# Attention in two float32r pieces, two heads in the row halves of TensorE, with the small steps of a group moved

## The reference

```python
# x: 8 sequences x 512 rows x 256; 16 heads of DH = 16
qkv = (x @ Wqkv).reshape(b, l, 3, H, DH)
q = q * cos + rotate_half(q) * sin          # the same for k
scores = einsum('bqhd,bkhd->bhqk', q, k) * DH ** -0.5
attn = softmax(scores, axis=-1)
out = einsum('bhqk,bkhd->bqhd', attn, v).reshape(b, l, d)
x = layernorm(x + out @ Wo)
x = layernorm(x + ffn(x))                   # shared expert + 2 of 8 experts
```

## Time and profile before

| | |
|---|---|
| Profiled execution, span of its instructions | 1291.3 us |
| Median of the three timed runs | 1292.8 us |
| PE / DVE / ACT / POOL busy over the span | 95% / 76% / 77% / 45% |
| Attention, from the first instruction to the last group | 0 to about 566 us |
| One group in the main loop | 64.06 us for four, 16.0 us each |
| Granted PE clock in the main loop | 0.99 to 1.00 |

### The profile page before, as it was taken

One profiled execution on the slowest core, in us unless ns is written; L12 is line 12 of the kernel. 1 busy time (PEld: TensorE's weight loads), 2 busy tenths in 40 slices (PEclk: granted clock), 3 DMA queues, 4 the chain that ended last, 5 costly groups with the idle time before them and its releaser, 6 DMA issues. The chain is left out here.

```text
span 1291.3 us, 29542 instructions
## 1 busy us (share of the span) xinstructions
PE 1224.3 (95%) x9440; PEld 934.5 (72%) x9440; DVE 976.6 (76%) x1925; ACT 996.4 (77%) x2043; POOL 583.9 (45%) x590
## 2 busy tenths in 40 slices
PE   4899999999999999979899969999999999999997
PEld 3444444444444444337899969999999999999897
DVE  6888887888788888728676648777777777777596
ACT  6699998999899999846654437777777777777687
POOL 6332322232223220005467745666666666666763
PEclk8899999999999999988899979999999999999999
DMA  9300000010000000433022246777777777776363
GB/s 298 117 19 19 18 19 20 2 35 3 19 2 19 2 18 3 144 104 117 18 91 100 87 158 197 260 251 253 246 238 238 235 249 253 253 239 217 101 218 119
DMA packets 125414, 161.28 MB, mean 125 GB/s; under 512 B 17088, under 2 KB 108224, under 8 KB 125312
## 3 DMA queue, kind: packets, MB, share of 16 engines
q1 hardware_dynamic: 118496, 141.25, 33.7%
q0 software_dynamic: 6816, 18.75, 4.1%
HBM read 122.06 MB, written 37.52 MB: 124 GB/s over the span
## 5 line engine op out<-in xcount | busy, mean ns | idle before, releaser
L546 DVE TENSOR_REDUCE att_mx<-att_psA 128x1 f32<-128x512 f32 x512 | 337.8, 683 | 75.5 <-PE att_psA L331 74.9
L461 ACT ACTIVATE att_prob<-att_psB 128x512 f32<-128x512 f32 x512 | 299.7, 600 | 54.0 <-PE att_psB L341 41.0
L341 PE MATMUL att_psB<-att_qk 128*128 128x512 bf16 x512 | 197.6, 388 | 12.8 <-issue 5.6
L1648 ACT ACTIVATE exp_psU<-exp_psU,ew_b 128x256 f32<-128x256 f32 x312 | 126.6, 447 | 103.7 <-PE exp_psU L1605 103.7
L331 PE MATMUL att_psA<-att_qk 96*128 96x512 bf16 x512 | 196.9, 386 | 3.0 <-DVE att_mx L546 3.0
L1699 DVE CAST exp_hh<-exp_psU 128x512 fp32r<-128x512 f32 x156 | 107.9, 692 | 101.9 <-ACT exp_psU L1648 101.9
L1588 PE MATMUL exp_psD<-exp_w2h,exp_hh 128*128 128x256 f32 x624 | 175.8, 282 | 0.0
L1603 PE MATMUL exp_psU<-exp_xh,exp_w1h 128*128 128x256 f32 x624 | 173.7, 278 | 1.4 <-DVE exp_xl L1690 1.4
L1605 PE MATMUL exp_psU<-exp_xh,exp_w1l 128*128 128x256 f32 x624 | 173.4, 278 | 0.0
L1604 PE MATMUL exp_psU<-exp_xl,exp_w1h 128*128 128x256 f32 x624 | 173.3, 278 | 0.0
L1589 PE MATMUL exp_psD<-exp_w2l,exp_hh 128*128 128x256 f32 x624 | 172.4, 276 | 0.0
(11 more groups left out here) (215 smaller groups left out, 3244.9 us busy)
## 6 DMA issues: line engine op xcount, KB each, us to landing
ew_w<-ew SPq DMA_DIRECT2D x40, 1024.0 KB, 6.1
exp_w<-ew SPq DMA_DIRECT2D x38, 1024.0 KB, 5.8
slots_x<-pre_acc SPq DMA_DIRECT2D x13, 780.0 KB, 10.8
pre_spare<-slots_x SPq DMA_DIRECT2D x39, 260.0 KB, 4.1
out_g<-rows_y SPq DMA_DIRECT2D x32, 256.0 KB, 4.1
ew_b<-eb SPq DMA_DIRECT2D x39, 128.0 KB
pre_spare<-xT SPq DMA_DIRECT2D x8, 512.0 KB, 4.5
attn_rows<-att_ob SPq DMA_DIRECT2D x8, 512.0 KB, 2.8
```

What stands on the lines that cost most here:

```text
L341: pe.matmul(psB[B_BANK[n % U]][:, :], r[:, 1, kt * P:(kt + 1) * P], r[:, 0, :], start=True, stop=True).then_inc(s_bmm, 1)
L461: act.activation(prob[:, n % PR, :], psB[B_BANK[n % U]][:, :], ACT.Exp, scale=SCALE).then_inc(s_exp, 1)
L546: dve.reduce_max(mx[:, g % 2, n % U:n % U + 1], psA[A_BANK[n % U]][:, :], AX_X).then_inc(s_max, 1)
```

## The change

The score operands become two float32r pieces (high and low), with three products of pieces, 3 x 16 = 48 rows, and the maximum in two pieces in rows 48 and 49 of the half. Two heads lie in the two halves of the 128 partitions (rows 0 to 63 and 64 to 127), so that a score product uses 64 rows of the array. In each unit the column product uses one half and the row product the other. A transposing step now turns a pair of heads, q or k, in four float32r products with a float32r identity (`turn_pair`), once in four units, and ACT copies 512 columns of it (`copy_pair`). POOL makes both pieces; the casts on DVE and the `spread` on ACT are gone. `split_max` is gone: `turn_max` transposes the maxima as float32, and `copy_max` cuts them in two on DVE, in two instructions, the second of which waits for the first. `place_max` issues four DMAs in place of three. The output has one buffer where it had two. The table of units is another, and the order in which psX is handed on is another.

```diff
-    TERMS = 6
+    TERMS = 3
     KR = TERMS * DH
+    PIECES = 2
+    KC = KR + PIECES
+    HALF = P // 2
-    PROJECT_QK, ROPE, COPY_OUT, TURN_OUT, NORM_OUT = (0, 1), (1, 2, 3), 3, 5, (5, 6)
-    PROJECT_V, COPY_V, SPLIT_MAX, TURN_MAX, COPY_MAX = 13, 13, 8, 10, 9
+    PROJECT_QK, TURN_MAX, TURN_OUT, PROJECT_V = (0, 4), 8, 10, 12
+    ROPE, COPY_MAX, NORM_OUT = (5, 6, 7), 9, (11, 12)
+    COPY_OUT, COPY_V, SPLIT_X = 4, 14, 12
...
+        qk = a.sb("qk", [P, RING, 2, PAIRS, L], F32R)
...
             def score_rows(n, it):
-                g, h, qt = n // U, n // NT, n % NT
+                g, u = n // U, n % U
+                pair, qt, j = u // (2 * NT), u // 2 % NT, 1 - u % 2
...
-                r = qk[0:KR, g % RING, :, h % G]
+                r = qk[half_of(j):half_of(j) + KR, g % RING, :, pair]
             def score_cols(n, it):
                 kt, j = u // G, u % G
...
-                r = qk[:, g % RING, :, j]
+                r = qk[half_of(j):half_of(j) + KC, g % RING, :, j // 2]
...
+            def turn_pair(k, it):
...
                 for t in range(NT):
+                    at = ((t * 2 + i) * H + h) * HALF
+                    m = pe.matmul(psT[:, t * P:(t + 1) * P], stack[:, b % 2, at:at + P], ident[:, :], start=True, stop=True)
+                m.then_inc(s_tmm, 1)
...
-                    last = {QK: (s_vev, p + V_LEAD, 1), OUT: (s_qrd, p + QK_LEAD + 1, 1),
-                            MAX: (s_onrm, p, 1), VALUE: (s_mev, p + 2, 1)}[use]
+                    last = {QK: (s_vev, p + V_LEAD, 1), MAX: (s_qrd, p + QK_LEAD + 1, 1),
+                            OUT: (s_mev, p + 2, 1), VALUE: (s_onrm, p, 1)}[use]
...
             def turn_max(g, it):
-                wait(pe, it, s_msp, g + 1, 1)
-                pe.matmul(psX[0:PIECES * U, 0:P], mstk[:, :, :].rearrange("p m u -> p (m u)"), ident[:, :], start=True, stop=True).then_inc(s_mtr, 1)
+                wait(pe, it, s_max, U * (g + 1), U)
+                pe.transpose(psX[:, 0:P], mx[:, g % 2, :], identf[:, :]).then_inc(s_mtr, 1)
...
             def place_max(g, it):
                 for k in range(PIECES):
+                    for j in range(2):
+                        row = half_of(j) + KR + k
...
             def copy_max(g, it):
-                dve.tensor_copy(mrow[:, g % 2, :], psX[0:PIECES * U, 0:P]).then_inc(s_mev, 1)
+                link(dve.tensor_scalar(mrow[:, g % 2, 0, :], psX[0:U, 0:P], -1.0, None, ALU.mult))
+                linked(it)
+                dve.scalar_tensor_tensor(mrow[:, g % 2, 1, :], psX[0:U, 0:P], -1.0, mrow[:, g % 2, 0, :].bitcast(F32),
+                                         ALU.mult, ALU.subtract).then_inc(s_mev, 1)
...
+            def split(tile, it):
...
+                    pool.tensor_tensor(rr[:, tile % 2, :], rc[:, :], rs[:, :], ALU.add).then_inc(s_rr, 1)
+                    for i in range(2):
+                        write_high(b, t, i, lambda out, *sides: pool.tensor_tensor(out, *sides, ALU.add), rc, rs).then_inc(s_hi, 1)
+                for i in range(2):
+                    wait(pool, it, s_hi, 2 * tile + i + 1, 2)
+                    pool.tensor_tensor(low(b, t, i), heads_of_part(rr[:, tile % 2, :], i), stacked(b, t, i)[:, :, 0:DH].bitcast(F32),
+                                       ALU.subtract).then_inc(s_lo, 1)
```

More of the change, by code:

```diff
@@ L152, in attention @@
         s_onrm = a.sem("o_normed")
[L153 to L156, removed]
+        s_ost = a.sem("o_stored")
+        s_tmm = a.sem("pair_turned")
+        s_tev = a.sem("pair_ready")
         s_mtr = a.sem("max_turned")
@@ L203, in heads_of, with stacked, half_of, high @@
             return t[:, :].rearrange("p (h d) -> p h d", d=DH)
-        def terms(stack, b, t):
-            return stack[:, b % 2, t].rearrange("p i h (m d) -> p (i h) m d", d=DH)
+        def stacked(b, t, i):
+            at = (t * 2 + i) * H * HALF
+            return stack[:, b % 2, at:at + H * HALF].rearrange("p (h m) -> p h m", m=HALF)
+        def half_of(j):
+            return HALF * (j % 2)
+        HI = ((0, 16), (0, 32))
+        LO = (32, 16)
+        def high(b, t, i):
+            first, second = HI[i]
+            return stacked(b, t, i)[:, :, first:second + DH].rearrange("p h (m d) -> p h m d", d=DH)[:, :, ::second // DH, :]
+        def low(b, t, i):
+            return stacked(b, t, i)[:, :, LO[i]:LO[i] + DH]
+        def heads_of_part(v, i):
+            return v[:, i * D:(i + 1) * D].rearrange("p (h d) -> p h d", d=DH)
+        def write_high(b, t, i, op, *sources):
+            return op(high(b, t, i), *(heads_of_part(v, i).unsqueeze(2).to_broadcast([P, H, 2, DH]) for v in sources))
         block = pr.block
@@ L461, in exps, with copy_pair @@
                 act.activation(prob[:, n % PR, :], psB[B_BANK[n % U]][:, :], ACT.Exp, scale=SCALE).then_inc(s_exp, 1)
-            def copy_head(h, it):
-                g = h // G
-                wait(act, it, s_tmm, h + 1, G)
-                act.activation(qk[0:KR, g % RING, :, h % G, :], psT[0:KR, :, :], ACT.Copy).then_inc(s_tev, 1)
+            def copy_pair(k, it):
+                g, pair, i = k // G, k % G // 2, k % 2
+                wait(act, it, s_tmm, k + 1, G)
+                act.activation(qk[:, g % RING, i, pair, :], psT[:, :], ACT.Copy).then_inc(s_tev, 1)
             def copy_out(g, it):
@@ L524, in period @@
                         copy_v(p + V_LEAD, it)
-                    if u == SPREAD and valid(p + QK_LEAD - 1, NT * B):
-                        spread(p + QK_LEAD - 1, it)
             groups(act, period)
@@ L601, in rope @@
                     wait(dve, it, s_rr, tile, 1)
+                    if tile > FILL:
+                        wait(dve, it, s_hi, 2 * tile, 2)
                     dve.tensor_tensor(heads_of(rc), x, table(cos, 0, DH), ALU.mult)
@@ L633, in _, with period @@
             dve.wait_ge(s_tab, 32)
-            def fill(tile):
+            def period(p, it):
+                tile = p + QK_LEAD
                 if tile < FILL:
@@ L654, in period @@
                         row_max(n + A_LEAD, it)
[L655 to L660 removed]
+                    if u in ROPE and valid(tile, NT * B):
+                        rope(tile, ROPE.index(u), it)
+                    if u == COPY_MAX and valid(p + 1, NG):
+                        copy_max(p + 1, it)
                     if u in NORM_OUT and valid(p - 1, NG):
                         norm_out(p - 1, NORM_OUT.index(u), it)
[L663 to L667 removed]
             def after_loop():
```

236 lines of the change are left out of this document (83 added, 153 removed).

## The result

The change makes the kernel 12.5% slower: 1458.8 us (median of four runs, 1441.6 to 1468.6) against 1293.0, a ratio of 1.125 [1.118, 1.131]. The forecast was 1331 us with a range up to 1375, so the direction was right and the size was missed by 128 us. The profiled execution spans 1457.1 us.

What follows compares the result with a forecast made beforehand. PE was taken as the bound, 16.1 us a group. The psX chain +31, store +14 and filling -6.5 gave +38.5 on 1291.3 us, 1330; the median, 1.5 higher, made it 1331 us, 8-in-10 range 1253 to 1375.

Steps and rivals of the forecast that it cites:

- PE's sum: PE's work per attention group: falls from 16.1 to 13.5 us, with 0.25 us for a pair of score products.
- the filling: Start of the kernel: first transpose at about 24 us, first column product some 6.5 us earlier (2 to 8).
- The chain through psX: Attention: four successive uses of psX make PE wait 3.7 us a group, 17.2 us a group in all, +31 us.
- The three waits: PE waits about 1 us each a group: output's transpose for maxima copy, v projection for norm_out, maxima's transpose for rope.
- the walk: Step-by-step timing of one attention period's hand-overs: PE works 13.5 us and waits 3.7, 17.2 us a group.
- Granted clock still near 1.00: Sign that the forecast is right: PE's granted clock stays near its full level.
- the slow clock: Rival: PE runs slow after each of seven store waits, some 4 us more each, +28, 1359 us; chance 0.07.
- The placing of the maxima behind the store: SP's queue in seven store periods: maxima land 2.0 us too late and block PE's first column product, +14 us.
- The halves do not overlap: Rival: a pair of score products costs 0.46 us, a group 18.8 us, +82, 1375 us; chance 0.17.
- PE's sum rules: Rival: waits in attention overlap more, so a group follows PE's work at 14.2 us, 1253 us; chance 0.17.

Runs made afterwards that it cites:

- e8: Kernel e1 with every score product over all 128 rows instead of half of them: 1300.3 us, ratio 1.007 to the kernel before.
- e5: Changed kernel with every score product over all 128 rows, same order and instructions: 1385.3 us, ratio 1.073 to the kernel before.
- e1: Changed kernel with half rows kept, but the units and psX order of the kernel before: 1307.4 us, ratio 1.016 to the kernel before.
- e9: Kernel e5 with the placing of the maxima ahead of the output store in SP's order: 1379.0 us, ratio 1.068 to the kernel before.
- e7: Changed kernel with the placing of the maxima ahead of the output store in SP's order: 1456.8 us, ratio 1.118 to the kernel before.
- e3: Kernel e1 with each unit's row product in the same row half as its column product: 1729.0 us, no ratio given.
- e2: Changed kernel with PE's waits filled: unit 10's row product issued five times, unit 12's turn three times: 1457.3 us, ratio 1.128 to the kernel before.
- e12: Changed kernel with the readers of psX ahead of each unit's row maximum on DVE: 1357.9 us, ratio 1.043 to the kernel before.

## Why the prediction was off, step by step

The medians split the loss into three steps: the float32r pieces in full rows and the old order, +10 us (e8 against the 1290.5 of before beside it); the order of psX at full clock, +85 (e5 against e8); the half rows in that order, +74 (after against e5). They sum to 168, against 166 measured, since before's own median moved from 1293.0 to 1290.5. The split depends on the order in which it is made: with the old order of psX the half rows cost 7 us (e1 against e8), not 74. The forecast had -72 for PE's sum and the filling, +110 for the chain and the store, and nothing for the clock.

- **The chain through psX: right.** The three waits are where the walk put them, 0.42, 1.08 and 1.02 us at full clock (the last in the wait list as 1.0). It gave 3.7 us of waiting a group; the order costs 3.0 (e5 against e8). The 2.5 us that PE's smaller sum was to pay back of them were not there.
- **PE's sum: the first step that failed, by the charge for borders.** I took 0.25 for a pair and 13.5 us a group; e1 has about 16. The price of the pair itself was right, 0.23 to 0.25 in a stream, and for the reason given, overlap, though the choice within 0.22 to 0.46 rested on column strips alone. What was mis-sized is the change of tile shape. I charged it for the turns only, eight changes and 0.6 us a group in all. It falls due wherever a half-row pair stands beside a full-array product, on both sides: e1 has twelve stays in the half rows (one or two pairs in a row), so that its sixteen pairs come to 6.1 us (8 x 0.43 + 4 x 0.67) in place of 4.0 and some 0.4 that the sum held with the products with V, and the full-array steps pay as well: q and k cost 0.84 to 0.90 in place of 0.7, the output's transpose 0.56 in place of 0.45. For v the new sum used 0.7, where the old sum had read 0.9 from the rows; it is 0.92. The rule of the Trainium skill, "TensorEngine Tiling (Array Packing)", section Key Properties, which I weighed in the prediction, was right in both halves: the tiles do run side by side, and a change of mode costs time, about 0.1 us on each side of a border in these traces. In the changed kernel's own order, with eight stays, I add the period from 261.62 to 280.48 up to 14.8 us of work, an estimate from the distances between starts; the other 4.1 of its 18.9 us are the three waits and smaller ones for exponents. The walk had 13.5 + 3.7. With 18.9 the term is 26 x (18.9 - 16.0) = +75 and not +31.
- **The granted clock: the second step that failed, and the larger.** "Granted clock still near 1.00" failed. I had the slow clock as a rival with 0.07 and +28 us, tied to waits of over 3 us. It fell behind waits of 1.1 us, once for 30 us in which PE was busy for 28.7, and is worth 74 us or somewhat more, since the half rows save 0.6 us a group at full clock. The earlier trace rows showed a fall behind a long wait, and I took the absence of long waits for safety; nothing in the trace of before had half the rows at work.
- **The placing of the maxima behind the store: mis-sized.** +14 was 7 x 2.0; e9 shows 6 us, 0.9 a store, in full rows. In the changed kernel PE waits for that DMA up to 3.1 us (685.64 us), but only in some periods, and e7 cannot resolve it.
- **The filling: wrong in sign.** First transpose at 24.48 us as forecast (24), but first column product at 55.62, against 52.45 before and some 46 forecast. With full rows the first column product comes earlier, at 50.87 in e8 and 48.82 in e5, so the pieces did save time there, and the half rows took more than it back: from 40 to 60 us their clock is 0.50 with PE busy for 17.8 of 20 us (row below), where before it was 0.83.
- **Rivals.** "The halves do not overlap" (1375) was wrong in mechanism, since they overlap fully, but nearer in size; that is luck, since the borders and the clock made up the difference. "PE's sum rules" failed with the sum.

```profile
40.00:60.00 20.00, 17.77 (x51) 10.46 (x50) 11.74 (x22) 2.89 (x6) 5.11 (x5) 0.50 0.21 66
```

What is open: what within a group brings the clock down and up again, and why four periods of the changed kernel pass without a fall. Shown are the ends: half rows with less overlap 0.50 (e3), column and row product at once without waits 1.00 (e1, 100 to 200 us), all rows with nearly the same waits 0.98 (e5). In between (after, e2, e12, and e1 itself behind the end of a pass) it changes sides, and I have no rule for when. Whether it is the rows in use or the number of products at work side by side that counts is not separated here.

## What to carry to other kernels

Price a change of tile shape at each border between small-tile and full-array products, not only in the new code: here the overlap was complete and the borders took back nearly all of it. Count the stays in the small tile, and put the small-tile products next to one another where the waits allow it. Where several steps share one bank, put its reader ahead of the bulk work on the reading engine, and keep uses some units apart; each hand-over that is followed at once costs its whole chain. And read the granted clock before believing a sum made at full clock: a trace without half-row products is no witness for the clock with them.

## What the runs showed of the hardware

- Two float32r products of 512 columns in two row halves cost no more than one: 0.42 to 0.43 us at full clock between other products (e1, a pair at 140.54, a single one at 550.99), 0.23 to 0.25 in a stream of half-row products (e2, 534.93; the second pair of a row in e1). In the full array two cost 0.46.
- A half-row product of 512 columns costs as much as a full-array one: 0.23 us in a stream at full clock (e2 and e8).
- A change between half rows and other products costs about 0.1 us on each side of the border at full clock (e1), and some 0.15 on the half-row side at 1.2 GHz (e3, 0.59 and 0.56 against 0.43).
- The granted clock was 0.50 from 100 to 760 us with PE busy all the time when the two half-row products of a unit shared a half (e3).
- It fell to 0.50 in the changed kernel behind waits of 0.4 and 1.1 us in six of ten periods, for 4 to 30 us, where full-row products with nearly the same waits kept 0.98 (e5). Behind like waits at the end of a pass it fell in e1 and stayed at 1.00 in e8.
